# Late layers of two token halves as two streams of twenty steps inside the slots of a chunked recurrence

## What is computed

```python
x = x + 0.5 * _L0_ffn_ref(_layernorm(x, axis=-1), L0_ffn_w_gate, L0_ffn_w_up, L0_ffn_w_down)
x = x + _L0_attn_ref(_layernorm(x, axis=-1), ...)
x = x + 0.5 * _L0_ffn_ref(_layernorm(x, axis=-1), L0_ffn_w_gate, L0_ffn_w_up, L0_ffn_w_down)
x = x + 0.5 * _L1_ffn_ref(_layernorm(x, axis=-1), L1_ffn_W_r, L1_ffn_W_k, L1_ffn_W_v, L1_ffn_mu_r, L1_ffn_mu_k)
x = x + _L1_attn_ref(_layernorm(x, axis=-1), L1_attn_Wqkv, L1_attn_Wout)
x = x + 0.5 * _L1_ffn_ref(_layernorm(x, axis=-1), L1_ffn_W_r, ...)
```

## Time and profile before

| what | value |
| --- | --- |
| time, median of 3 runs (lowest, highest) | 7938.85 us (7925.99, 7946.14) |
| the profiled execution's own time | 7923.61 us |
| its span, first to last instruction | 7921.5 us |
| busy share PE, DVE, ACT, POOL | 81%, 58%, 33%, 29% |
| mean granted clock of PE, share of full | 0.901 |

### The profile page before, as it was taken

One profiled execution on the slowest core, in us unless ns is written; L12 is line 12 of the kernel. 1 busy time (PEld: TensorE's weight loads), 2 busy tenths in 40 slices (PEclk: granted clock), 3 DMA queues, 4 the chain that ended last, 5 costly groups with the idle time before them and its releaser, 6 DMA issues. The chain is left out here.

```text
span 7921.5 us, 162593 instructions
## 1 busy us (share of the span) xinstructions
PE 6393.1 (81%) x60192; PEld 4617.5 (58%) x60192; DVE 4580.4 (58%) x9651; ACT 2614.0 (33%) x5275; POOL 2274.8 (29%) x3893
## 2 busy tenths in 40 slices
PE   7787887877878788787878878788787887878776
PEld 4565656656565565655656566565655656556564
DVE  6556564655656546565565746557565465755653
ACT  3224242332424224242242423324242252423321
POOL 2414223141321413224142331413214132241321
PEclk9898898989989898898988989899898998989898
DMA  1100001001010110001100110011001100111000
GB/s 52 28 36 21 26 30 36 28 21 38 25 28 28 27 43 21 22 32 27 39 21 26 31 34 28 21 38 31 22 28 27 43 21 22 33 25 39 21 27 3
DMA packets 376536, 226.37 MB, mean 29 GB/s; under 512 B 336896, under 2 KB 353920, under 8 KB 367488
## 3 DMA queue, kind: packets, MB, share of 16 engines
q1 hardware_dynamic: 375680, 215.29, 9.4%
HBM read 156.54 MB, written 58.72 MB: 27 GB/s over the span
## 5 line engine op out<-in xcount | busy, mean ns | idle before, releaser
L1562 PE MATMUL PS<-BIG 32*32 32x32 f32 (+3 forms) x23744 | 1095.7, 258 | 330.4 <-PEq L1708 194.8
L800 DVE SCALAR_TENSOR_TENSOR PS<-BIG,CW,PS 128x512 f32<-128x512 f32 x1536 | 1155.9, 753 | 203.5 <-DVEq L798 125.2
L1562 PEld LDWEIGHTS PS<-BIG 64*64 64x64 f32 (+2 forms) x23744 | 913.9, 135 | 514.5 <-issue 500.4
L1562 PE MATMUL PS<-XT,BIG 128*128 128x512 f32 x2048 | 1048.3, 644 | 49.7 <-PEq L1885 49.7
L1565 PE MATMUL PS<-CST,BIG 128*128 128x128 f32 x3536 | 602.2, 312 | 536.2 <-PEq L1638 209.8
L1565 PEld LDWEIGHTS PS<-CST,BIG 128*128 128x128 f32 x3536 | 447.1, 158 | 684.4 <-issue 668.8
L1062 POOL TENSOR_TENSOR RSTD<-VAR,NHALF 128x2 f32<-128x2 f32 x202 | 141.9, 702 | 1981.7 <-POOLq L1061 1981.7
L1562 PEld LDWEIGHTS PS<-XT,BIG 128*128 128x128 f32 x2048 | 390.4, 202 | 386.1 <-issue 377.5
L1562 PE MATMUL PS<-BIG,CST 128*128 128x256 f32 (+1 forms) x1360 | 499.3, 512 | 102.0 <-PEq L1955 95.6
L1223 POOL TENSOR_TENSOR FR<-MS,NHALF 128x8 f32<-128x8 f32 x128 | 209.9, 1640 | 1249.6 <-POOLq L1222 982.2
L1145 POOL TENSOR_TENSOR BIG<-BIG 128x30 f32<-128x30 f32 (+14 forms) x960 | 517.2, 539 | 136.4
(11 more groups left out here) (148 smaller groups left out, 9994.9 us busy)
## 6 DMA issues: line engine op xcount, KB each, us to landing
BIG<-in_wv SPq DMA_DIRECT2D x16, 2048.0 KB, 7.5
BIG<-in_wo SPq DMA_DIRECT2D x16, 2048.0 KB, 7.5
BIG<-in_wq SPq DMA_DIRECT2D x16, 1024.0 KB, 4.9
BIG<-in_wk SPq DMA_DIRECT2D x16, 1024.0 KB, 7.5
cells_in<-BIG SPq DMA_DIRECT2D x128, 128.0 KB, 2.7
BIG<-cells_in SPq DMA_DIRECT2D x32, 512.0 KB, 3.7
cells_out<-BIG SPq DMA_DIRECT2D x32, 512.0 KB, 3.2
cells_nat<-BIG SPq DMA_DIRECT2D x32, 512.0 KB, 4.1
```

The source lines that it names most:

```text
L800: op = v.scalar_tensor_tensor(y, pre[:, j:j + G], CW[:, i * TAPS + j:i * TAPS + j + 1], y, ALU.mult, ALU.add)
L1562: return nc.tensor.matmul(out_, l, r, start=start, stop=stop)
```

## The change

Three edits. (1) `FILL` becomes one step in each of the three places of all eight chunks, 24 slots in all. (2) The late layers of each half become a generator `late(h)` of twenty steps on PE, ACT and POOL and twice twenty on DVE. Half 0's steps stand in slots 1 to 20, those of half 1 in slot 3 and in slots 5 to 23, so that most slots hold one step of each half. Slot 0 has the last two `gate_up`, slot 1 `down(1)`. (3) Since the halves now overlap, they get buffers of their own: half 1's stand in `AT`, `KQ` and `PT_ALL`, in the parts of chunks 0 to 3, which are read no more by then. `XT` is laid out as halves with a leading column each, for which DVE copies two more columns per mix of half 0.

```diff
-FILL = [(2, 2, 2)] * 5 + [(1, 1, 1)] * 3 + [(0, 0, 0)]
+FILL = [(1, 1, 1)] * CHUNKS + [(0, 0, 0)]
+SLOTS = 3 * CHUNKS
+LATE_AT = ((*range(1, 21),), (3, *range(5, 24)))
...
+    order += [f"g0{m}" for m in range(HT)] + ["g10", "d0", "g11", "g12", "g13"]
+    for n in range(SLOTS):
+        order += {0: ["g14", "g15"], 1: ["d1"]}.get(n, [])
+        for h in range(2):
+            if n in LATE_AT[h]:
+                order += late_steps(h).get(LATE_AT[h].index(n), [])
...
-        VTOK, VBD, KM = tl(5120, 2 * D), tl(1024, 2 * G), tl(5632, 2 * G)
-        SCB, PT = [tl(G * i, G) for i in range(2)], [tl(3072 + G * i, G) for i in range(2)]
-        OB, OT = VTOK, QT
+        VBD = (tl(512, 2 * G), AT[:, 0:2 * G])
+        QT, KTT = (XK, AT[:, 1024:1536]), (KA, AT[:, 1536:2048])
+        KM = (tl(4608, 2 * G).rearrange("p (b t) -> p b t", b=16), KQ[:, :].rearrange("p (b t) -> p b t", b=16)[:, :, 0:BLK])
+        SCB = [[tl(at + G * i, G) for i in range(2)] for at in (3584, 2560)]
+        PT = [PT_ALL[:, G * i:G * i + G] for i in range(2)]
+        OB = (VTOK, PT_ALL[:, 1024:1536])
...
+                streams = late(0), late(1)
+                for n in range(SLOTS):
+                    if n == 0:
+                        gate_up(1, 4)
+                        gate_up(1, 5)
+                    if n == 1:
+                        down(1)
+                    for h in range(2):
+                        if n in LATE_AT[h]:
+                            next(streams[h])
+                    if n == SLOTS - 1:
+                        for free in ring_free:
+                            pe.wait_ge(free, 1)
+                            pe.sem_inc(free, -1)
+                    yield
```

```diff
+                    now = [streams[h] for h in range(2) if n in LATE_AT[h]]
+                    for s in now:
+                        next(s)
+                    if n == 2:
+                        normal(1, x, TXN, txn_ready)
+                    for s in now:
+                        next(s)
+                    yield
```

More of the change, by code:

```diff
@@ L304, in bass_macaron @@
         km_ready = sem("km_ready")
-        km_used = sem("km_used")
+        km_used = [sem(f"km_used{h}") for h in range(2)]
         sc_ps = sem("sc_ps")
@@ L1128, in tail @@
                     yield
+                    yield
+                    yield
+                    yield
+                    yield
+                for m in range(HT):
+                    yield
+                rstd(0)
                 yield
@@ L1132, in tail @@
                 yield
-                yield
+                streams = late(0), late(1)
+                for n in range(SLOTS):
+                    if n == 1:
+                        rstd(1)
+                    for h in range(2):
+                        if n in LATE_AT[h]:
+                            next(streams[h])
+                    yield
             cells = M.rearrange("p (j i) -> p j i", j=SUB)
@@ L1264, in xt_copy @@
                 act.sem_inc(xt_ps_act, -1)
-                a.activation(XT[:, 1:G + 1], bank(0), ACT.Copy).then_inc(xt_act, 1)
+                a.activation(XTH[:, 0, :, 1:HG + 1], v3(bank(0), 2), ACT.Copy).then_inc(xt_act, 1)
             def ffn():
@@ L1384, in tail @@
                     yield
-                squared(0, 1)
-                yield
-                yield
-                transposed("x1u")
-                yield
-                squared(1, 1)
-                yield
-                yield
+                    transposed(f"x{h}u")
+                    yield
+                    yield
+                    squared(h, 1)
+                    yield
+                    yield
+                for m in range(HT):
+                    gate(0, m)
+                    yield
+                for m in range(4):
+                    gate(1, m)
+                    yield
+                streams = late(0), late(1)
+                for n in range(SLOTS):
+                    if n == 0:
+                        gate(1, 4)
+                        gate(1, 5)
+                    for h in range(2):
+                        if n in LATE_AT[h]:
+                            next(streams[h])
+                    yield
             def tanh_of(i):
@@ L1833, in tail @@
                     yield
-                shift(0, 1)
-                yield
-                values(0, 1)
-                yield
-                transposed("x1u")
-                yield
-                shift(1, 1)
-                yield
-                values(1, 1)
-                for free in ring_free:
-                    pe.wait_ge(free, 1)
-                    pe.sem_inc(free, -1)
-                yield
+                    transposed(f"x{h}u")
+                    yield
+                    yield
+                    shift(h, 1)
+                    yield
+                    values(h, 1)
+                    yield
+                copied(2)
+                for m in range(HT):
+                    gate_up(0, m)
+                    yield
+                gate_up(1, 0)
+                down(0)
+                yield
+                for m in range(1, 4):
+                    gate_up(1, m)
+                    yield
+                streams = late(0), late(1)
+                for n in range(SLOTS):
+                    if n == 0:
+                        gate_up(1, 4)
+                        gate_up(1, 5)
+                    if n == 1:
+                        down(1)
+                    for h in range(2):
+                        if n in LATE_AT[h]:
+                            next(streams[h])
+                    if n == SLOTS - 1:
+                        for free in ring_free:
+                            pe.wait_ge(free, 1)
+                            pe.sem_inc(free, -1)
+                    yield
             def after_conv(i):
```

401 lines of the change are left out of this document (163 added, 238 removed).

## The result

The changed kernel takes 7722.1 us (median of 4 runs, 7708.5 to 7743.2) against 7932.4 us for the kernel before (4 runs, 7926.0 to 7946.1). The ratio is 0.9735, interval [0.9712, 0.9758]. The forecast was 7375 us with a range of 7140 to 7620. The sign was right; 210 us came between the medians (198 between the two profiled spans) where 563 were forecast, and the time lies 102 us above the range.

What follows compares the result with a forecast made beforehand. No engine is full (PE busy 81%), so PE's waits were taken as what reordering can reach. 16 x (23 + 10) plus 35 = 563 us off gave a median of 7375 us, range 7140 to 7620.

Steps and rivals of the forecast that it cites:

- (a): Recurrence: dependent steps of one half come a slot later, so of 42 us late-layer PE waits per block 23 go.
- (b): Recurrence: PE's low-clock stretches shrink with its waits, giving 10 us per block, bounds 3 and 17.
- (d): Chunk 3: POOL's inverse reaches PE by scatter too late, a 4 us wait already counted among the remaining 19.
- (c): Last block's late layers: 30 us of waits covered by the other half, 5 us by clock; 35 us once, bounds 15 and 55.
- (e): Two narrow DVE copies per block and the gapped `XT` and `KM` layouts cost nothing; at most 1.6 us per block.
- The second: Rival: DVE's queue becomes the bound in chunks 3 and 4; only 12 us waits, 5 clock go; 7647 us, chance 0.14.
- The third rival: POOL's substitution, held by DVE instructions, makes the scatter 35 us later; about 7936 us (chance 0.02) or 8015 us (0.04).
- The rival that the ring ties the streams: Three-bank ring makes one half's steps wait for the other's reader; 5 us counted, chance within the DVE queue rival's 0.14.
- The no-change and slower cases: POOL and scatter as bound: no change, about 7936 us, chance 0.02; with further POOL waits slower, 8015 us, chance 0.04.

Runs made afterwards that it cites:

- x12: x11 with DVE's `normalise` and `right_side` of chunk 7 ahead of both late steps, `values(0, 1)` and `mix(1, 1)`, of slot 20; 7512.2 us, 0.9454.
- x13: x11 with only `mix(1, 1)` of slot 20 put behind DVE's `right_side` of chunk 7, `values(0, 1)` staying ahead of `normalise`; 7506.6 us, 0.9451.
- x16: x2 with only DVE's `right_side` of chunk 7 put ahead of `mix(1, 1)` in slot 20; 7562.8 us, 0.9520.
- x14: x13 with, in slot 17 too, DVE's `mix(0, 1)` put behind the `right_side` of chunk 6; 7516.6 us, 0.9462.
- x15: x14 with, in slots 11 and 14 too, half 1's softmax put behind the `right_side` of chunks 4 and 5; 7636.8 us, 0.9615.
- x2: The changed kernel with POOL's substitution for chunks 4 to 7 one piece earlier in POOL's order; 7621.3 us, 0.9623.
- x17: The kernel before the change with POOL's substitution one piece earlier; 7928.0 us, 0.9990.
- x11: x6 plus PE's late step ahead of `inverse_t(1, 1)` in slot 12 and DVE's `scaled(1, 3)` ahead of `mix(0, 1)` in slot 17; 7575.3 us, 0.9554.
- x6: x2 with the ring reordered so slot 14's scores need no bank that DVE's `scaled(0, 3)` frees; 7626.0 us, 0.9610.
- x9: x11 plus DVE's `normalise` ahead of the late step in slot 20 alone; 7617.0 us, 0.9605.
- x5: x2 with DVE's `normalise` ahead of the late step in slot 20 alone; 7670.2 us, 0.9660.
- x3: The changed kernel with DVE's `normalise` ahead of the third slot's late step in all chunks; 7928.6 us, 1.0002.
- x4: x2 with DVE's `normalise` ahead of the third slot's late step in all chunks; 7841.9 us, 0.9898.
- x10: x6 plus DVE's `scaled(1, 3)` ahead of `mix(0, 1)` in slot 17; 7631.8 us, 0.9619.

## Why the prediction was wrong

**(a) The order in the recurrence** failed, and not where I had marked the doubt. I walked through the slots for late-layer waits and put 19 us down to what is left; the rows give 17.3 us, or 22.9 with the scatter, which I had counted in. The failed step is "42 - 19 = 23 us per block go". It holds the recurrence's own waits at the 7.6 us of before. In the block shown they are 16.9 without the scatter: 9.2 for `normalise`, 4.7 and 1.9 for ACT's copies of the inverse (L2113, L2158) and some short ones. PE's idle time fell from 50 to 39.8 us, 10 instead of 23 (51.8 to 39.5, 12 us, in the mean of the blocks). The walk was right for chunks 0 to 2: I had 3, 4 and 2 us of waits there, and PE is idle for 3.8, 3.0 and 1.9 us. In chunks 3 to 7 I had 10 us of late waits; PE is idle for 31 us, and chunks 4 to 7 are together 10 us *longer* than before. In each chunk DVE's late step of the third slot stands between `s_update` and the next `right_side`. That it lies on the path that sets the chunk is shown for slot 20 by x12, x13 and x16, at 58 to 69 us of the time. For slot 17 x14 finds 1.4 us of idle time per block and no gain; for slots 11 and 14 it is not shown, and x15 shows that their softmax rounds cannot just be put back. The other half of what chunks 3 to 7 lost is PE's busy time, most of it by the clock, see (b).

**(d) The scatter** was sized 4 us; the wait is 5.6. Its price is larger than the wait: x2 took 6.7 us off chunk 3, 5.4 of idle time and 1.3 of busy time at a clock that rose from 0.81 to 0.85. The failed part is "the shorter chunks 0 to 2 bring PE there some 25 us sooner". They do (27), but `inverse_q(1, 0)` also moved from some 23 to 9 us behind chunk 3's start, as the late step before it went from two to one. PE came 42 us sooner, the scatter 20. Against a slack of 16 that is 6 us, as measured. x17 shows no gain to be had before.

**(b) The clock** failed too. In the block shown PE's busy time fell by 4.2 us (186.49 to 182.31), which would be within my bounds of 3 to 17, but in the mean of the 14 blocks it rose by 0.4 us and the clock stayed at 0.88 to 0.89: nothing came where 10 us per block, 160 in all, were forecast. The failed step is "if the low stretches shrink as the waits do". A quarter of the idle time went and no part of the low clock did; it moved from chunks 1 and 2 to chunks 4 and 6. The price per wait is real in single places: in x13's chunk 7 2.1 us of idle time went and 1.6 us of busy time with them. But x11 gained 3.0 us of busy time with hardly any idle time gone, and x14 lost 1.7 us where 1.4 of idle time went. So idle time in all does not tell the clock; what does was not found.

**(c) The last late layers** gave 14 us, not 35 and just under my bound of 15. PE's idle time there went from 65.6 to 49.5 us, 16 less where 30 were forecast, and its busy time rose by 2.2 us where the clock was to give 5. L1661 (normalised x) and L1655 (`claim`) still hold 35 us. "I take 30 as covered by the other half" is the failed part. Why half of it stayed is open; no run was made on it.

**(e) What was added** cost nothing: DVE's busy time in the recurrence is 123.37 us for 123.14. The matmuls of `scores` with half 1's `KM` (KQ,BIG, 64x256) take 376 ns in the median where the granted clock is full, and those of half 0, with the old layout, 376 as well; at the lower level both take 631.

**The rivals.** The second, DVE's queue, came nearest (12 us of waits and 5 of clock per block, 7647 us; 12 and none came in the mean of the blocks), and I gave it 0.14. Its tell-tale was wrongly chosen, though. I asked for DVE busy over 75% of the recurrence with waits at `r_ready`. DVE is busy 56%, and PE stands at `normal_out`, one step ahead of `r_ready` in PE's order. In slot 20, where it was tested, it is the order in DVE's queue that binds, not its load; I had used "busy only 52%" as evidence against it, and that is no evidence. The third rival did not come as told: POOL's substitution operations take 549 and 541 ns in the recurrence for 607 and 538, so DVE's instructions do not hold them longer than before. (The Trainium skill, page SBUF — State Buffer, section "Who interferes with whom", says that a VectorE instruction with two SBUF inputs contends with a GpSimd instruction that reads SBUF. The meeting of the earlier trace rows agrees, 0.69 to 1.51 us, but no cost of it changed here.) The row that I called "alone" was no such thing: it ran beside a POOL operation, from 3247.31 us on, that took 0.82 us where the two of its line around it took 0.45 and 0.35. There POOL seems to have been the one that was held. It was POOL's order, not its speed, that made the scatter late. The rival that the ring ties the streams is there in one place, at the 5 us that I had put down to it: the longest wait of L1714 (4.9 us) is half 1's scores at the bank that half 0's `scaled` frees, and in x6 it went (119 to 42 us at that line over the whole run, x2 to x6). Nothing was gained by it. The no-change and slower cases are excluded by the interval.

Put together: 16 x 11.9 for the recurrence, 14 once at the end, 4 in the stretch ahead of the first recurrence (276.2 to 272.3), less 16 x 0.8 for the rest: 195, against 198 us between the two spans. Against the forecast (a) fell short by 16 x 10.7 = 171 us, (b) by 16 x 10.4 = 166 and (c) by 21. Of (a) the runs show the cause for most: 101 us by the scatter (x2) and 58 to 69 by the late step of slot 20 (x12, x13, x16). For (b) and (c) they show that the gain did not come, and the cause is open.

## What to carry to other kernels

When waits are spread over two streams, list the waits of the *other* chain too: an engine that runs both in order will put the one's steps on the other's path. Ask of each late step on a helper engine who stands behind it in that queue, and put it behind the result that the bottleneck engine needs next, if its own reader is a slot or more away; and keep it as cover where the queue would wait anyway (`values(0, 1)` before the power). Where a stretch gets shorter, add up all that PE has no longer ahead of a transfer's first use, not only the stretch itself. And a PE wait removed alone proves little: four of them gave nothing one by one. Before a gain is put down to waits, split it into idle and busy time: x11's 46 us looked like waits that had gone and were nearly all the clock.

## What the runs showed of the hardware

The granted clock costs or gives 40 us between kernels in which PE waits the same time. x9 and x11 differ in one `normalise` on DVE; their recurrences are 213.3 and 212.9 us. But the rest of the period, which neither edits, is 248.8 against 246.1 us in the mean, and the medians are 42 us apart. The same stretch in one block of x9, then of x11:

```profile
3266.90:3517.60 250.70, 216.08 (x1297) 138.12 (x1298) 157.06 (x281) 107.35 (x232) 85.18 (x167) 0.88 0.12 35
```

```profile
3245.10:3488.00 242.90, 205.03 (x1298) 131.56 (x1299) 156.62 (x280) 107.25 (x232) 84.65 (x167) 0.94 0.13 36
```

The matmuls are the same within the records (1297, 1298) and take 11 us longer at 0.88. In the mean of the blocks they take 5.0 us longer (212.2 and 207.3 us), while PE is idle for 2.3 us less. Over the blocks the rest takes 240 to 256 us in nearly every kernel here; in most of them about two thirds of the blocks stay under 248 us, in x9 and x5 nearly all take 248 to 252. x5 against x2 is the same picture: recurrences of 216.5 us in both, the rest 248.9 against 245.5, and 49 us in the medians.

This is not chance from run to run. Each of these four kernels keeps its time within 6 to 31 us over its four runs, and the two with the long rests are just the two that put `normalise` ahead of the late step in slot 20 alone. So the 42 and 49 us go with that edit, in a stretch that it does not touch. By what way it would lower the clock there was not found; no run was aimed at it. (x12 also puts `normalise` ahead in slot 20, with `right_side` behind it, and x3 and x4 do so in all chunks; their rests are 246.0, 247.5 and 246.2 us.)

The same split for the other kernels, in us per block:

| | recurrence | PE idle in it | PE busy in it | its clock | rest |
| --- | --- | --- | --- | --- | --- |
| before | 234.7 | 51.8 | 182.9 | 0.884 | 245.5 |
| after | 222.8 | 39.5 | 183.3 | 0.885 | 246.3 |
| x2 | 216.5 | 34.6 | 181.9 | 0.892 | 245.5 |
| x5 | 216.5 | 34.5 | 182.1 | 0.894 | 248.9 |
| x10 | 216.4 | 34.3 | 182.1 | 0.886 | 246.4 |
| x11 | 212.9 | 34.0 | 178.9 | 0.917 | 246.1 |
| x9 | 213.3 | 34.4 | 178.9 | 0.918 | 248.8 |
| x13 | 209.2 | 31.9 | 177.3 | 0.924 | 245.2 |
| x14 | 209.4 | 30.5 | 179.0 | 0.916 | 246.3 |
| x16 | 213.3 | 32.6 | 180.8 | 0.896 | 245.7 |

For reading such experiments it means that a difference of 50 us can be the clock alone, without any more waiting, and that the recurrence's own length, and its idle and busy time, have to be looked at beside the median.
